# Three layers in one program block, idle TensorE time filled with transposes, and a mask moved ahead of a sigma

## The chip, the cores and the metric

The kernel runs on one core of one Trainium2 chip. The metric is the time of one execution on the device, in microseconds (us); less is better. A core has five engines that work side by side, each through its own list of instructions in order: TensorE (PE in the profile, its weight loads PEld), VectorE (DVE), ScalarE (ACT), GpSimd (POOL) and SyncE (SP), which here only issues transfers. An engine waits for another by a semaphore: the one counts it up at the end of an instruction, the other stands before an instruction until the count is reached. A float32 matmul here runs in passes over a 128 × 128 stationary operand. TensorE's clock has two levels, 1.2 and 2.4 GHz, and the profile shows the granted share of the full one: 0.5 is 1.2 GHz.

## What is computed

1024 tokens of 256 numbers pass through four layers, each taken of the normalised x and added to x. Cut to what matters:

```
x = x + delta_attention(layernorm(x))   # 16 heads of 128, segments of 64 tokens, a memory per head
x = x + mixture0(layernorm(x))          # "e0": 16 experts, 2 picked per token, and a shared expert
x = x + retention(layernorm(x))         # one head: Q, K turned by cos/sin tables, scores times a decay
x = x + mixture1(layernorm(x))          # "e1": 8 experts, the best one per token, weighted
```

In the first layer, per segment: `scores = q kT / sqrt(128)` masked causally, a softmax, `att_dot = softmax @ v`; `att_mem = sigma(q) @ mem / (sigma(q) @ z)` with `sigma(a) = elu(a) + 1`; then `mem += sigma(k)T @ (v - sigma(k) @ mem / (sigma(k) @ z))` and `z += sum of sigma(k)`. The output is a mix of the two by a sigmoid per head, times Wo. In the third layer, `Q = xpos(x W_Q)`, `K = xpos(x W_K)`, `att = (Q KT * D) V` with D a lower triangular decay.

## The kernel before

**The tiling.** Tokens lie in NT = 8 tiles of 128 partitions; a half is TPH = 4 tiles, 512 tokens. Float32 products that need precision are made of three matmuls, `split3` (L213 to L215), of a high and a low part of each operand. `Norm` serves the layernorm of every layer n (0 to 3) in halves: `statistics` and `normalise` (L132) on VectorE, `invert` (L112, the power −0.5) on GpSimd, `turn` (L140, eight transposes against the identity, two groups of four) on TensorE, `high` (L149, a copy) on ScalarE and `low` (L157, the difference) on VectorE. Each counts a semaphore, and the next waits for it.

**Attention** takes four heads at a time (`it`) and one half of the tokens (`half`): 8 stages, n = 0 to 7. A stage has 8 segments (STEPS) for two groups of two heads, so 16 recurrence steps, and behind each step `slot(it, half, m, ...)`, m = 0 to 15, issues other work on every engine: projections and sigma of the next stage ("ahead"), softmax and reading of this one. The order is written out by hand, in `AHEAD_AT` and in the slots' conditions. On VectorE `sigma(n + 1, ..., u)`, u = 0 to 7 (queries, then keys), is L869, L875 and, for keys, the copy L880; at m = 7 it is unit 5, the key of head 1. `mask_scores` (L907 and the row maximum L912) runs at m = 1 and m = 7, once for each pair of heads. TensorE's turn of the probabilities of the first pair into the bank `local` is L594, its turn of a key's sigma L554; ScalarE's L749 and L750 copy a projection (its exponent's input, and q or k) from a bank and L758 copies a turned sigma from one.

**The sparse layers** (`sparse_layer`, tag e0 or e1) turn the normalised rows, make router logits (`logits`, L1255 in e1), count the tokens of each expert (L1295 to L1302), number the slots (L1310), and then work through blocks of 128 gathered rows: a gather (L1195, GpSimd), a turn (L1331), gate and up (L1340, 128 × 352), the hidden's turn (L1350), down (L1358) and a scatter (L1206, GpSimd). `number_shares` (L1320) brings each row's weight into block order. In e0, SyncE reads the scattered results back and VectorE joins them to x (`join`, L1113): four calls, (half, k); (1, 1) is left to the retention (`join_last`).

**The retention** splits its three weights on GpSimd (`w_high` L1791, `w_low` L1795), projects Q and K in four units (`project`), multiplies each by cos and sin (`products`, L1921 and L1922 on VectorE), combines them on GpSimd (L1806), splits the outcome (L1885 on ScalarE, L1929 on VectorE), and makes scores and outputs tile by tile.

**What sets the order between layers.** Each of the four layers is an `nc.Block()`. At its end every engine drains (L1120) and all meet at a barrier; GpSimd's drain counts among them. Inside a block each engine works through what its function issues, in that order.

Of the kernel before, what the change touches and what calls it, by code (L numbers as in the profile page):

```python
# [165 lines left out]
class Carried:  # L166
# [3 lines left out]
    def __init__(self, nc, ctx):  # L170
# [9 lines left out]
        self.y_last = [flat[:, i * D:(i + 4) * D].rearrange("p (t d) -> p t d", d=D) for i in (12, 0)]  # L180
        self.tile_loaded = [sem(f"first_tile{i}_loaded") for i in range(2)]
# [3 lines left out]
class SharedTiles:  # L185
# [32 lines left out]
def delta_attention(nc, outer, norm, carried, x, ident, ident_ready, scratch, x_in, Wq, Wk, Wv, Wo, betas, mask_in,  # L218
# [12 lines left out]
    with ExitStack() as ctx:  # L231
# [114 lines left out]
        with nc.Block() as block:  # L346
# [497 lines left out]
            def _(dve):  # L844
# [58 lines left out]
                def mask_scores(n, before):  # L903
                    if before:
# [5 lines left out]
                       .then_inc(masked, 1)  # L910
                    dve.wait_ge(masked, n + 1)
# [77 lines left out]
def sparse_layer(nc, outer, norm, carried, x, ident, ident_ready, tag, experts, picks, w, tiles=None, next_w=None,  # L989
                 out=None, signals=()):  # L990
# [7 lines left out]
    with ExitStack() as ctx:  # L998
# [31 lines left out]
        consts = sb("consts", [P, table.shape[1]])  # L1030
# [7 lines left out]
        router = sb("router", [P, KD, E])  # L1038
# [45 lines left out]
        router_loaded, table_loaded, weights_loaded = sem("router_loaded"), sem("table_loaded"), sem("weights_loaded")  # L1084
# [23 lines left out]
        def join(engine, half, k):  # L1108
# [3 lines left out]
            for t in range(half * TPH, (half + 1) * TPH):  # L1112
                last = engine.scalar_tensor_tensor(  # L1113
# [6 lines left out]
        with nc.Block() as block:  # L1120
            @block.sync
            def _(sp):
# [3 lines left out]
                if out is not None:  # L1126
                    for half in range(2):
                        sp.dma_start(rows[half * HALF:(half + 1) * HALF, D:2 * D].rearrange("(t p) d -> p t d", p=P),
                                     x[:, half * TPH:(half + 1) * TPH, :]).then_inc(rows_stored, 16)
                if shared:  # L1130
                    tiles.load(sp, stage[2], 2, stage_loaded)
                for e in range(E):
                    sp.dma_start(weights[:, e, :], w["experts"][e, :, :]).then_inc(weights_loaded, 16)
                if shared:
                    for i in range(3):
                        sp.dma_start(carried.retention_w[i], next_w[i].rearrange("(k p) n -> p k n", p=P))\
                          .then_inc(carried.retention_w_loaded[i], 16)
                for ring in range(RING):
                    sp.wait_ge(scattered[ring], 16 * scatters(ring))
                if out is None:  # L1140
                    for half in range(2):
                        if half:
                            sp.wait_ge(y_loaded[0], 16 * K)
                        for k in range(K):
                            first = k * T + half * HALF
                            sp.dma_start(y[k][half], results[first:first + HALF, :].rearrange("(t p) d -> p t d", p=P))\
# [931 lines left out]
```

## Time and profile before

| | |
|---|---|
| time, median of 3 runs | 738.09 us (735.9 to 738.6) |
| the profiled execution | 737.92 us |
| its span, first to last instruction | 736.1 us |
| mean granted TensorE clock | 0.948 |
| busy TensorE, VectorE, ScalarE, GpSimd | 651.0, 401.8, 340.0, 317.1 us |
| attention | to 451.5 us |
| e0 | 451.5 to about 598 us |
| retention | 601.5 to about 656 us |
| e1 | 658.4 to 736 us |

The span is 1.8 us shorter than the execution, which has work around it. In the rows further down a line of a timeline is one instruction or a run of equal ones: its start, how long it was busy, engine, line, what it wrote and read; in square brackets how long the engine had idled before it, and what released it.

### The profile page before, as it was taken

The numbers are of one execution on the slowest core, as the hardware profiler recorded it, in microseconds if no ns is written. First come the engines' busy times: TensorE is split into PE (matmuls) and PEld (weight loads), VectorE is DVE, ScalarE is ACT, GpSimd is POOL, SyncE is SP. The second block draws the span as 40 slices with busy tenths as digits, with TensorE's granted clock in tenths as the row PEclk, the third lists the DMA queues.
The fourth block names the chain that finished last, engine by engine and source line by source line (L and its number), as shares of the span: only waits on it lengthen the run. The fifth ranks groups of instructions, "written<-read, shape, count | busy, mean of one in ns | idle before, by whom it ended". The sixth has DMA issues, their size and how long they took to land. (4 is left out here: it accounts for less than half of the span.)

```text
span 736.1 us, 12298 instructions
## 1 busy us (share of the span) xinstructions
PE 651.0 (88%) x4144; PEld 543.3 (74%) x4144; DVE 401.8 (55%) x1055; ACT 340.0 (46%) x834; POOL 317.1 (43%) x383
## 2 busy tenths in 40 slices
PE   4888999999999999999999987999999519984897
PEld 3777888989979979989889886875666317873564
DVE  6768396295394493691772737862222178354243
ACT  3565767467566565665765642233333203100210
POOL 4565562454353344436420204246665318111563
PEclk9999999999999999999999998999999859995799
DMA  8011010200200100100100414953232241019440
GB/s 265 23 54 34 29 55 5 63 31 2 65 29 22 44 28 28 36 28 29 37 1 1 115 53 137 415 189 93 93 91 76 100 148 53 1 56 341 134 124 15
DMA packets 31313, 57.89 MB, mean 79 GB/s; under 512 B 4670, under 2 KB 17952, under 8 KB 31264
## 3 DMA queue, kind: packets, MB, share of 16 engines
q1 hardware_dynamic: 24256, 42.03, 16.7%
q0 software_dynamic: 4896, 13.12, 6.1%
q10 hardware_dynamic: 2112, 2.10, 0.8%
q8 instruction: 29, 0.48, 0.3%
q14 instruction: 20, 0.16, 0.1%
HBM read 48.06 MB, written 10.09 MB: 79 GB/s over the span
## 5 line engine op out<-in xcount | busy, mean ns | idle before, releaser
L891 DVE RECIPROCAL denominators<-readings 128x2 f32<-128x2 f32 x128 | 21.1, 165 | 147.6 <-PE readings L567 146.6
L427 POOL TENSOR_TENSOR w_high<-xn,ones 128x256 fp32r<-128x256 f32 x84 | 53.9, 673 | 78.2 <-PE ahead L215 35.4
L567 PEld LDWEIGHTS readings<-memory_copy,sigma 128*128 128x128 f32 x512 | 75.2, 191 | 11.2 <-ACT memory_copy L764 2.1
L773 ACT ACTIVATE memory_reading<-readings,denominators 64x128 f32<-64x128 f32 x256 | 78.5, 356 | 6.0 <-DVE denominators L891 4.0
L567 PE MATMUL readings<-memory_copy,sigma 128*128 128x129 f32 x512 | 78.7, 275 | 2.2 <-ACT memory_copy L764 2.1
L764 ACT ACTIVATE memory_copy<-memory 128x258 f32<-128x258 f32 x128 | 50.2, 393 | 62.1 <-PE memory L577 48.1
L897 DVE SCALAR_TENSOR_TENSOR minus_delta<-readings,denominators,v 64x128 f32<-64x128 f32 x240 | 73.8, 347 | 4.5 <-DVE denominators L891 0.3
L577 PE MATMUL memory<-minus_delta,sigma_k_tokens 128*128 128x129 f32 x480 | 73.2, 275 | 0.0
L1195 POOL DMA_INDIRECT xs_e<-rows_e,gather_at_e x46 | 44.8, 974 | 58.4 <-DVE scatter_at_e L1596 36.1
L1340 PE MATMUL up_e<-weights_e,xT_e 128*128 x184 | 68.7, 497 | 0.8 <-ACT xT_e L1464 0.8
L431 POOL TENSOR_TENSOR w_low<-xn,w_high 128x256 fp32r<-128x256 f32 x84 | 65.7, 812 | 1.6
L616 PE MATMUL ahead<-wo,attT 128*128 128x256 f32 x256 | 64.5, 396 | 1.0 <-DVE attT L926 1.0
L749 ACT ACTIVATE x<-ahead 128x512 f32<-128x512 f32 x60 | 35.9, 598 | 61.5 <-PE ahead L215 28.3
L1681 DVE TENSOR_TENSOR h_e<-gated_e,up_e 128x176 f32<-128x176 f32 x46 | 15.5, 337 | 88.4 <-ACT gated_e L1471 88.4
L577 PEld LDWEIGHTS memory<-minus_delta,sigma_k_tokens 128*128 128x128 f32 x480 | 63.0, 191 | 0.0
L458 POOL TENSOR_TENSOR xn<-scores,exp_sum_inverse 64x512 f32<-64x512 f32 x32 | 34.1, 1065 | 60.8 <-DVE exp_sum_inverse L918 59.1
L616 PEld LDWEIGHTS ahead<-wo,attT 128*128 128x128 f32 x256 | 58.9, 306 | 1.3 <-DVE attT L926 1.2
L1358 PE MATMUL down_e<-weights_e,hT_e 128*128 (+1 forms) x184 | 56.3, 405 | 0.0
L213 PE MATMUL ahead<-xh,w_high 128*128 128x512 f32 x120 | 52.4, 437 | 1.9 <-POOL w_low L431 1.9
L449 POOL TENSOR_TENSOR scores<-scores,score_max 128x512 f32<-128x512 f32 x16 | 16.7, 1047 | 82.3 <-DVE score_max L912 76.6
L1340 PEld LDWEIGHTS up_e<-weights_e,xT_e 128*128 128x128 f32 x184 | 32.2, 195 | 24.9 <-issue 15.6
L215 PE MATMUL ahead<-xh,w_low 128*128 128x512 f32 x120 | 47.4, 395 | 0.0
(267 smaller groups left out, 1424.8 us busy)
## 6 DMA issues: line engine op xcount, KB each, us to landing
weights_e<-experts SPq DMA_DIRECT2D x24, 608.0 KB, 12.0
xn<-L_attn_Wq SPq DMA_DIRECT2D x8, 512.0 KB, 3.9
xn<-L_attn_Wk SPq DMA_DIRECT2D x7, 512.0 KB, 3.8
xn<-L_attn_Wv SPq DMA_DIRECT2D x7, 512.0 KB, 3.8
wo<-L_attn_Wo SPq DMA_DIRECT2D x1, 2048.0 KB, 13.1
rows_e<-xn ACTq DMA_DIRECT2D x4, 512.0 KB, 10.6
x<-L_attn_x SPq DMA_DIRECT2D x4, 256.0 KB, 3.5
x<-L_attn_x SPq DMA_DIRECT2D x2, 512.0 KB, 3.5
```

Of the source, the lines that this page charges most:

```text
L213: pe.matmul(out, sh, mh, start=first, stop=False, **kw)
L215: return pe.matmul(out, sl, mh, start=False, stop=last, **kw)
L427: last = pool.tensor_tensor(w_high[i][:, :, of], w_stage[:, :, of], one, ALU.mult)
L431: last = pool.tensor_tensor(w_low[i][:, :, of], w_stage[:, :, of], fr(w_high[i][:, :, of]), ALU.subtract)
L567: last = pe.matmul(KQ[g][:, hh * MC:(hh + 1) * MC], sqk[:, GROUP * g + hh, pair, 2 * par:2 * par + 2, :], mz[g][:, hh, :], start=True, sto ...
L577: last = pe.matmul(MM[g][:, hh * MC:(hh + 1) * MC], skt[:, GROUP * g + hh, pair, :], dl[g][par][:, hh, :], start=False, stop=True, skip_gr ...
L616: last = pe.matmul(A[1][:, 0:D], rows[:, i::H], wo[:, i, :], start=(i == 0), stop=(i == H - 1))
L764: act.activation(mz[g][:, :, :], MM[g][:, 0:GROUP * MC].rearrange("p (h c) -> p h c", h=GROUP), ACT.Copy).then_inc(mem_copied[g], 1)
L773: last = act.activation(read[rows, half, GROUP * g + hh, pair, :], KQ[g][rows, hh * MC:hh * MC + DK], ACT.Copy, scale=nr[g][rows, hh:hh + 1])
L897: last = dve.scalar_tensor_tensor(out=dl[g][par][rows, hh, 0:DK], in0=KQ[g][rows, hh * MC:hh * MC + DK], scalar=nr[g][rows, hh:hh + 1], in ...
L1340: last = pe.matmul(GU[b % 2][:, 0:2 * INTER], xT[b % 2][:, k, :], flat[:, bass.ds(first + k * 2 * INTER, 2 * INTER)], start=k == 0, stop=k ...
L1358: last = pe.matmul(Y[b % 2][:, 0:D], hT[b % 2][0:count, k, :], flat[0:count, bass.ds(first + 4 * INTER + k * D, D)], start=k == 0, stop=k ...
```

## The change

It has four parts.

1. **Attention.** `mask_scores` loses the row maximum, which becomes `row_maxima`. At m = 7 the mask is issued ahead of sigma unit 5, the row maximum stays behind it. At m = 1 nothing moves.
2. **Merged layers.** e0, the retention and e1 are bodies of one block, made with `no_gpsimd_drain=True`: no drain and no barrier stands between them, and none of GpSimd behind them. Three waits order what the barriers did: SyncE's loads of the retention's tables wait for the read-back of e0 (`read_back`), e1's row stores wait for the retention's last addition (`earlier_done`), and e1's router and table are loaded inside the retention, into `carried`, once its second normalise is done.
3. **Filled time.** `busy` issues transposes of the identity into a bank that nobody reads: 16 before and 14 after the retention's first turn, 16 after e1's first logits, 8 after its second turn, 34 after its slot numbers.
4. **Order.** Both inversions of the retention's layernorm stand on GpSimd behind its weight splits (the first one was in e0). VectorE's last two joins are cut in halves, around a normalise and around a `low`. TensorE projects the second unit before the second turn, not behind it; `number_shares` comes behind the first block's gate and up matmuls.

The diff, with changed indentation left out:

```diff
+def busy(pe, bank, ident, count):
+    for _ in range(count):
+        pe.transpose(bank[:, 0:P], ident[:, :], ident[:, :])
...
+                def row_maxima(n):
                     dve.wait_ge(masked, n + 1)
                     dve.tensor_reduce(mx[:, :], sm[:, :, :], AX.X, ALU.max).then_inc(max_ready, 1)
...
                     ahead, behind = not (last and half), not (first and not half)
+                    if m == 7:
+                        mask_scores(2 * n + 1, True)
                     if ahead:
...
+                    if m == 1:
+                        mask_scores(2 * n, behind)
                     if m in (1, 7):
-                        mask_scores(2 * n + m // 7, behind or m == 7)
+                        row_maxima(2 * n + m // 7)
...
-        with nc.Block() as block:
             @block.sync
             def _(sp):
+            if out is None:
                 sp.dma_start(router[:, :, :], w["router"].rearrange("(k p) e -> p k e", p=P))\
                   .then_inc(router_loaded, 16)
                 sp.dma_start(consts[:, :], table).then_inc(table_loaded, 16)
-                if out is not None:
+            else:
+                sp.wait_ge(earlier_done, 4)
...
-                if out is None:
-                    norm.invert(pool, N + 1, 0)
...
                     logits(0)
+                busy(pe, acc[0], ident, 16)
                     norm.turn(pe, N, 1, acc)
+                busy(pe, acc[0], ident, 8)
                     logits(1)
                     count_tokens()
                     number_slots()
+                busy(pe, acc[0], ident, 34)
...
-                if out is not None:
-                    number_shares()
                 turn_rows(0)
                 turn_rows(1)
...
                         block_gate_up(b, firsts[b])
+                if out is not None and b == 0:
+                    number_shares()
...
-                    join(dve, 1, 0)
+                join(dve, 1, 0, (0, 1))
                     norm.normalise(dve, N + 1, 0)
+                join(dve, 1, 0, (2, 3))
...
+            sp.wait_ge(read_back, 16 * K0)
                 for i, t in enumerate(tables):
                     sp.dma_start(cos_sin[:, i, :], t).then_inc(tables_loaded, 16)
                 sp.dma_start(decay[:, :], decay_in).then_inc(decay_loaded, 16)
+            sp.wait_ge(norm.xn_done, NT * 2 + TPH)
...
-                    if i == 0:
-                        pool.wait_ge(w_split, 1)
-                        norm.invert(pool, 2, 1)
-                        pool.wait_ge(norm.xn_done, NT * 2 + NT)
+            for half in range(2):
+                norm.invert(pool, 2, half)
...
-                pe.wait_ge(ident_ready, 2)
+            pe.wait_ge(norm.stats_done, NT * 2 + 1)
+            busy(pe, B[7], ident, 16)
                 norm.turn(pe, 2, 0, B[0:4])
+            busy(pe, B[7], ident, 14)
...
                 project(0)
-                norm.turn(pe, 2, 1, B[0:4])
                 project(1)
+            norm.turn(pe, 2, 1, B[0:4])
...
-                join_last(dve)
+            join_last(dve, (0, 1))
                 norm.low(dve, 2, 0, B[0:4])
+            join_last(dve, (2, 3))
...
+        with nc.Block(no_gpsimd_drain=True) as block:
```

**Where the instructions stand.** VectorE in an attention stage's slot 7, before. `x` is the exponent that sigma caps, `scores` the masked scores, `score_max` the row maxima, `local0` the bank of the raw scores:

```order
L897 SCALAR_TENSOR_TENSOR minus_delta11<-readings1,denominators1,v 64x128 x2
L869 TENSOR_SCALAR x<-x 128x512
L875 SCALAR_TENSOR_TENSOR sigma_k1<-kT,x 128x512
L880 COPY sigma<-sigma_k1 128x4x2x64
L907 SCALAR_TENSOR_TENSOR scores<-local0,mask 128x512
L912 TENSOR_REDUCE score_max<-scores 128x8
```

The same place after:

```order
L908 SCALAR_TENSOR_TENSOR minus_delta11<-readings1,denominators1,v 64x128 x2
L918 SCALAR_TENSOR_TENSOR scores<-local0,mask 128x512
L880 TENSOR_SCALAR x<-x 128x512
L886 SCALAR_TENSOR_TENSOR sigma_k1<-kT,x 128x512
L891 COPY sigma<-sigma_k1 128x4x2x64
L925 TENSOR_REDUCE score_max<-scores 128x8
```

The mask has moved up over the three instructions of one sigma, and the row maximum has not.

GpSimd from e0's last scatters to the retention's rotations, before (`rstd` is an inversion; `w_low_r` and `w_high_r` are the weight splits):

```order
L1206 DMA results_e0<-ys2_e0,scatter_at_e0 6016x256
L112 TENSOR_TENSOR rstd<-var_eps,power 128x4
L1120 UNCONDITIONAL_BRANCH
L1784 UNCONDITIONAL_BRANCH
L1786 MEMSET ones_r 128x1
L1795 TENSOR_TENSOR w_low0_r<-carried,w_high0_r 128x512
L112 TENSOR_TENSOR rstd<-var_eps,power 128x4
L1791 TENSOR_TENSOR w_high1_r<-carried,ones_r 128x512
L1795 TENSOR_TENSOR w_low1_r<-carried,w_high1_r 128x512
L1791 TENSOR_TENSOR w_high2_r<-carried,ones_r 128x512
L1795 TENSOR_TENSOR w_low2_r<-carried,w_high2_r 128x512
L1806 TENSOR_TENSOR turned0_r<-product0_r 128x512 x2
```

The same place after:

```order
L1228 DMA results_e0<-ys2_e0,scatter_at_e0 6016x256
L1813 UNCONDITIONAL_BRANCH
L1815 MEMSET ones_r 128x1
L1824 TENSOR_TENSOR w_low0_r<-carried,w_high0_r 128x512
L1820 TENSOR_TENSOR w_high1_r<-carried,ones_r 128x512
L1824 TENSOR_TENSOR w_low1_r<-carried,w_high1_r 128x512
L1820 TENSOR_TENSOR w_high2_r<-carried,ones_r 128x512
L1824 TENSOR_TENSOR w_low2_r<-carried,w_high2_r 128x512
L112 TENSOR_TENSOR rstd<-var_eps,power 128x4 x2
L1833 TENSOR_TENSOR turned0_r<-product0_r 128x512 x2
```

The block's end (L1120) is gone from between them, and both inversions stand behind all five splits.

TensorE at the front of e1, before:

```order
L1777 UNCONDITIONAL_BRANCH
L1229 UNCONDITIONAL_BRANCH
L140 MATMUL down_e<-ident,xn 128x128 x8
L1255 MATMUL routing_e<-router_e,turned_e 128x8 x8
L140 MATMUL down_e<-ident,xn 128x128 x8
L1255 MATMUL routing_e<-router_e,turned_e 128x8 x8
```

The same place after:

```order
L1249 UNCONDITIONAL_BRANCH
L140 MATMUL down_e<-ident,xn 128x128 x8
L1275 MATMUL routing_e<-carried,turned_e 128x8 x8
L218 MATMUL down_e<-ident 128x128 x16
L140 MATMUL down_e<-ident,xn 128x128 x8
L218 MATMUL down_e<-ident 128x128 x8
L1275 MATMUL routing_e<-carried,turned_e 128x8 x8
```

L218 are the transposes of the identity: they stand between the first logits and the second turn, and between that turn and the second logits.

## Rows read from the trace of the kernel before

**Rows 1.** The page's line of the granted TensorE clock, in 40 slices, in tenths.

```profile
PEclk9999999999999999999999998999999859995799
```

**Rows 2.** Waits, 60 to 540 us: who waited for whom, us, times, longest.

```profile
PE local L594 <- DVE scores L907: 6.2, 7, 2.7
```

**Rows 3.** Timeline of an ordinary attention stage: start, duration, engine, line, [idle <-releaser].

```profile
270.06 0.69 DVE L907 SCALAR_TENSOR_TENSOR scores<-local,mask 128x512 f32<-128x512 f32 x1
270.06 0.60 ACT L749 ACTIVATE x<-ahead 128x512 f32<-128x512 f32 x1 [0.67 <-DVE sigma L880]
270.55 0.59 ACT L750 ACTIVATE kT<-ahead 128x512 f32<-128x512 f32 x1
...
270.81 1.09 PE L594 MATMUL local<-ident,xn 128*128 128x128 f32 x8 [0.57 <-DVE scores L907]
271.03 0.60 ACT L758 ACTIVATE sigma_k_tokens<-ahead 128x512 f32<-128x512 f32 x1
...
271.74 0.60 PE L554 MATMUL ahead<-ident,sigma_k 128*128 128x128 f32 x4
...
272.09 0.48 PE L213 MATMUL ahead<-w_high,xh 128*128 128x512 f32 x1
```

**Rows 4.** Timeline of the first attention stage.

```profile
64.47 0.60 ACT L749 ACTIVATE x<-ahead 128x512 f32<-128x512 f32 x1 [2.06 <-DVE sigma L880]
...
65.30 0.69 DVE L907 SCALAR_TENSOR_TENSOR scores<-local,mask 128x512 f32<-128x512 f32 x1 [0.93 <-POOL xn L458]
...
66.14 1.86 PE L594 MATMUL local<-ident,xn 128*128 128x128 f32 x8 [2.72 <-DVE scores L907]
...
67.80 1.06 PE L554 MATMUL ahead<-ident,sigma_k 128*128 128x128 f32 x4
```

**Rows 5.** The drains that end a block: durations min/median/max in ns.

```profile
L1120 SPq DRAIN  x2: 7/64/122, 590.4 to 734.8; - x2
L1120 POOLq DRAIN  x2: 3757/5000/6242, 595.0 to 732.2; - x2
```

**Rows 6.** Timeline from the first sparse layer to the retention.

```profile
595.16 1.67 DVE L1113 SCALAR_TENSOR_TENSOR x<-y_e,carried,x 128x256 f32<-128x256 f32 x4 [0.24 <-DMA carried<-results_e]
...
601.57 2.68 DVE L1113 SCALAR_TENSOR_TENSOR x<-carried,x 128x256 f32<-128x256 f32 x4 [3.43 <-PEq L1120]
...
605.62 0.79 PE L213 MATMUL bank_r<-xh,w_high_r 128*128 128x512 f32 x1 [2.05 <-DVE xl L157]
```

**Rows 7.** Timeline of the retention: rotary products, rotations, first score matmul.

```profile
612.53 0.68 DVE L1921 TENSOR_TENSOR product_r<-bank_r,cos_sin_r 128x512 f32<-128x512 f32 x1
...
614.74 6.06 POOL L1806 TENSOR_TENSOR turned_r<-product_r 128x512 f32<-128x512 f32 x4
...
627.15 0.50 PE L213 MATMUL bank_r<-q_high_r,k_high_r 128*128 128x512 f32 x1 [0.43 <-DVE q_low_r L1929]
```

**Rows 8.** Timeline from the retention to the second sparse layer.

```profile
655.28 1.38 DVE L132 TENSOR_SCALAR xn<-x,mean_var,rstd 128x256 f32<-128x256 f32 x4 [0.16 <-POOL rstd L112]
...
658.55 1.06 PE L140 MATMUL down_e<-ident,xn 128*128 128x128 f32 x8 [2.40 <-PEq L1777]
...
660.45 3.55 PE L1255 MATMUL routing_e<-router_e,turned_e 128*128 128x8 f32 x16 [0.83 <-ACT turned_e L1437]
```

**Rows 9.** Windows: us, busy PE PEld DVE ACT POOL, PEclk, DMA share, GB/s.

```profile
70.00:72.00 2.00, 2.00 (x16) 1.86 (x16) 0.80 (x4) 0.98 (x2) 0.00 (x0) 1.00 0.00 0
...
660.00:661.00 1.00, 0.56 (x3) 0.58 (x3) 0.26 (x3) 0.30 (x1) 0.63 (x1) 0.58 1.02 302
```

**Rows 10.** Timeline of the second sparse layer, up to its third block.

```profile
677.11 0.39 PE L1310 MATMUL routing_e<-token_e,in_slot_e 128*128 128x30 bf16 x8 [4.43 <-DVE token_e L1581]
...
684.32 0.69 PE L1331 MATMUL routing_e<-ident,xs_e 128*128 128x128 f32 x2 [0.79 <-DMA xs_e<-rows_e,gather_at_e]
...
685.82 2.71 PE L1340 MATMUL up_e<-weights_e,xT_e 128*128 x4 [0.81 <-ACT xT_e L1464]
...
691.43 1.35 PE L1340 MATMUL up_e<-weights_e,xT_e 128*128 x4
```

More of the change, by code:

```diff
@@ L1029, in sparse_layer @@
         table = w["table"]
-        consts = sb("consts", [P, table.shape[1]])
+        consts = carried.next_table if out is not None else sb("consts", [P, table.shape[1]])
         at = table_columns(E, K)
@@ L1106, in sparse_layer, with join @@
         turned_done = sem("turned_done")
-        def join(engine, half, k):
+        def join(engine, half, k, part=range(TPH)):
             engine.wait_ge(y_loaded[half], 16 * K)
@@ L1111, in join @@
                 engine.wait_ge(joined, (half * K + k) * TPH)
-            for t in range(half * TPH, (half + 1) * TPH):
-                last = engine.scalar_tensor_tensor(
+            for t in (half * TPH + i for i in part):
+                engine.scalar_tensor_tensor(
                     out=x[:, t, :], in0=y[k][half][:, t - half * TPH, :], scalar=share[:, k, t:t + 1],
@@ L1134, in _ @@
-                if shared:
[L1135 to L1139, printed above, removed]
-                if out is None:
[L1141 to L1146, printed above, removed]
-                              .then_inc(y_loaded[half], 16)
@@ L1727, in join_last @@
-    def join_last(engine):
-        join(engine, 1, 1)
-        engine.wait_ge(joined, 2 * K * TPH)
-    return join_last
-def retention(nc, outer, norm, carried, x, ident, ident_ready, tables, decay_in, join_last):
+            else:
+                sp.wait_ge(earlier_done, 4)
+                for half in range(2):
+                    sp.dma_start(rows[half * HALF:(half + 1) * HALF, D:2 * D].rearrange("(t p) d -> p t d", p=P),
+                                 x[:, half * TPH:(half + 1) * TPH, :]).then_inc(rows_stored, 16)
@@ L1740, in retention, with join_last @@
+    def join_last(engine, part):
+        join(engine, 1, 1, part)
+        if TPH - 1 in part:
+            engine.wait_ge(joined, 2 * K * TPH)
+    return join_last, y_loaded[1]
+def retention(block, nc, outer, norm, carried, x, ident, ident_ready, tables, decay_in, join_last, read_back, next_w):
     with ExitStack() as ctx:
@@ new lines, in _, with high, copy_v @@
+        @block.scalar
+        def _(act):
+            act.wait_ge(w_loaded[0], 16)
+            act.activation(w_high[0][:, :, :], w_stage[0][:, :, :], ACT.Copy).then_inc(high_done, 1)
+            for half in range(2):
+                norm.high(act, 2, half, B[0:4])
+            def high(u):
+                qk, half = units[u]
+                act.wait_ge(turn_done, 2 * u + 2)
+                act.activation(qk_high[qk][:, :, half * HALF:(half + 1) * HALF], turned[u % 2][:, :, :], ACT.Copy)\
+                   .then_inc(qk_high_done, 1)
+            def copy_v(b):
+                act.wait_ge(v_ready, 2 * b + 2)
+                act.activation(v[:, 2 * b:2 * b + 2, :], B[4 + b][:, :].rearrange("p (t d) -> p t d", t=2), ACT.Copy)\
+                   .then_inc(v_copied, 1)
+            high(0)
+            high(1)
+            copy_v(0)
+            copy_v(1)
+            high(2)
+            copy_v(2)
+            copy_v(3)
+            high(3)
@@ L1965, in build @@
+        return added
 def build(nc, ins, out):
```

1340 lines of the change are left out of this document (669 added, 671 removed).

## Prediction

> **What bounds the kernel now.** Three views are read, in this order. The page's line of the granted TensorE clock comes first: nearly full in the attention stages (the first 451 us, 24 slices), at half in slice 33 (589 to 607 us: the end of the first sparse layer and the front of the retention), and at 5 and 7 tenths in slices 37 and 38 (662 to 699: the front of the second sparse layer) [rows 1]. Those dips are the places that the merge and the fillers touch. The waits of the attention stages come next: the matmul that turns the second pair's probabilities (L594) waits for the mask (L907) on VectorE seven times, 6.2 us in total, 2.7 of it once [rows 2]. The timelines around each changed place are last. In attention TensorE is busy nearly all the time, so an instruction that reaches it late is paid; behind attention the path runs from engine to engine, and each edit is read from the wait that ends last there. All is worked against the profiled execution, 737.92 us, of which the span is 736.1 and 1.8 lie around it. It is 0.2 below the median of the runs shown (738.09), so a change of the one is a change of the other.
>
> **Attention, +3.1 us.** In an ordinary stage the mask ends at 270.75, the turn L594 starts at 270.81 having idled 0.57, takes 1.09, and the key's turn L554 follows at 271.74, the projection of the next stage at 272.09 [rows 3]. With the mask first, L594 no longer idles, but the key's sigma ends 0.72 later (0.69 and a gap). Three things hang on that sigma. ScalarE's copy L749 is released by it: 270.06 becomes 270.78. The copy L750 behind it reads the bank that L554 writes, and ends at 271.86 instead of 271.14; L554 then starts at about 271.90, not 271.74, though TensorE is free 0.57 sooner. The copy L758 ends at 272.35 instead of 271.63, and the projection's bank waits for it: 272.40 instead of 272.09, +0.31. So the removed wait comes back on the next two instructions, with 0.31 on top. Six such stages are +1.9. In the first one the mask had to wait 0.93 for GpSimd's L458, until 65.30, while the sigma before it had let L749 go at 64.47 [rows 4]. The sigma now queues behind that wait: it starts when the mask ends, at 65.99, and L749 behind it moves by some 2 us. TensorE idled there anyway until 66.14 [rows 4], so the end that all of it hides is +0.4 and the end that all is paid is +2.1; +1.2 is taken, the middle, for nothing decides. The last stage has no sigma. The sum is 1.9 + 1.2 = +3.1. Were the waits simply to go and nothing to take their place, it would be at best 6 × 0.57 = −3.4, say −3.5; the upper bound, with the first stage at its upper end and 0.4 per stage, is +4.5.
>
> **First sparse layer to retention, −4.2 us.** GpSimd's drain starts at 595.0 and takes 6.2 [rows 5]; the other engines stand at the barrier until 601.4, VectorE for 3.43 [rows 6]. Without it the order is: the last inversion, then the first two joins (0.42 each, 1.67 for four [rows 6]), normalise at 596.1 for 1.38 (as long as in [rows 8]), the turn on TensorE at 597.5. The 16 transposes ahead of it fill idle time, and the 14 behind it lie beside ScalarE's two copies and VectorE's differences; the other joins cost 0.42, not 0.67 (2.68 for four [rows 6]), because no split runs beside them. The first projection starts at 600.5 instead of 605.62 [rows 6]. Two units of projection run before the second turn (24 matmuls, to 606.0), and VectorE is free for the rotary products at 608.5 instead of 612.53 [rows 7]. GpSimd takes them up at 609.8 instead of 614.74: it was behind the weight splits, which now lie in its idle time before 595. From there eight rotations set the pace; a little slower beside products, they deliver the last at about 622.7 where the first score matmul stood at 627.15 [rows 7], −4.4. TensorE, done earlier, now idles some 2.8 us before the scores where it idled 0.43, and may lose its clock: 0.2 is set aside, and the bounds are −4.6 and −2.9 (1.7 for a stretch at 1.2 GHz). The new wait of SyncE, for the read-back, is over when the joins start at 595.16, and the tables then have 12 us to land. That the second turn now stands behind the second projection is in the 608.5.
>
> **Front of the second sparse layer, −2.1 us.** The normalise ends at 656.66, and the turn came at 658.55, released by the barrier [rows 8]; it now comes at 656.7, and the first logits at 658.5 instead of 660.45, −1.95. The clock was at 1.2 GHz in 660 to 661, after this idling [rows 9], and the 16 logits matmuls took 3.55 [rows 8] without raising it. The 16 transposes cost 16 × 0.135 = 2.2 at the upper level (1.06 for eight [rows 8]) and 16 × 0.23 = 3.7 at the lower (1.86 for eight [rows 4]); the next 8 lie beside ScalarE's copies (0.83 of idle ahead of the first logits [rows 8]) and cost 0.3 net. At the upper level the second turn takes 0.9 less and the second logits about 1.7 less, half of 3.55, an estimate. If the clock falls in the first logits and is up again by the end of the 16: −1.95 + 3.7 + 0.3 − 0.9 − 1.7 = −0.6. If it never falls, the first logits save 1.7 too: −1.95 + 2.2 + 0.3 − 0.9 − 3.4 = −3.8. About the middle is taken. Router and table are now loaded in the retention; no row here waits for them, so that is nothing. Upper bound 0.
>
> **First expert blocks, −1.8 us.** The slot numbers are done at 677.5, and until the first rows land TensorE has the 24 share matmuls and nothing else; the second set is turned at 684.32, the first gate and up matmuls start at 685.82 and take 2.71, where the same takes 1.35 at 691.43 [rows 10]. The 34 transposes start at 677.5; with the clock low for the first 3.5 (in attention it was low from 66.14 and full from 70 on [rows 4, 9]) they are done at 683.6 (15 × 0.23, 19 × 0.135), before the second set's rows at 684.32. Then the first two blocks run at the upper level: 2 × 1.35 saved, less 0.5 for the 24 share matmuls, now between them, and less what the blocks wait for ScalarE's table load; the third block starts at 689.7 instead of 691.43. Bounds: −2.2, and +1.4, when the clock rises late.
>
> **The end, −1.1 us.** GpSimd's drain from 732.2 takes 3.8, to 736.0; SyncE, which waits for the stores of the result, is done at 734.8 [rows 5]. Bounds 0 and −1.1.
>
> **Sum.** 3.1 − 4.2 − 2.1 − 1.8 − 1.1 = −6.1, so 731.8 for the profiled execution and 732.0 beside the median.
>
> **A rule against it.** From 66.14 on TensorE had turns alone, eight in 1.86 at the lower level and four more to 68.9 [rows 4], and from 70 to 72 the clock was full [rows 9], so turns may help to raise it. The Trainium skill, "TensorE: Matmul & The Clock Gate", Part 4 (PE-mode transpose), says that such a transpose "doesn't count as PE-busy the same way". By it the fillers would be pure cost, as in rival 2.
>
> **Rivals.** 1: *the attention's wait goes and nothing takes its place* (the copies turn out not to hold the banks that I think). Attention −3.5 in place of +3.1: 731.8 − 6.6 = 725.2, so 725.4 beside the median. For it: L594's wait is real. Against it: L749 is released by the sigma in both stages shown [rows 3, 4]. Chance 0.07. 2: *the fillers do not raise the clock* and end above the kernel before. The retention's front keeps −1.2, since 14 transposes at 0.23 hold its first projection back by 3.2 and only the rotations' earlier start is left; the second layer's front is −1.95 + 24 × 0.23 − 0.7 = +2.9; 34 × 0.23 = 7.9 puts the first turned rows to 685.4, and with the shares behind them that is +2.1; attention +3.1, end −1.1. The sum is +5.8, 744. It decides from the point at which the 34 end later than the rows land, 684.3, which is 0.20 per transpose. For it: the first logits kept the clock low for all their length [rows 8]. Against it: the turns of [rows 4]. Chance 0.09. 3: *the clock falls in the longer idle of the retention, or rises late in the second layer*: retention −2.9, front 0, blocks −0.3 or worse: 735 to 737. For it: idling of 2.4 was enough before 660 [rows 8, 9], and 2.8 are expected here. Chance 0.19. 4: *a data wait takes the barrier's place* (the read-back, the splits or the stores end as late as the drain did), and with attention's loss nothing is left: 738. Against it: the joins' data had landed at 595.16 [rows 6]. Chance 0.05. The forecast keeps 0.60.
>
> **How the numbers follow.** The likeliest is 732.0. Its own range, from the bounds of the terms that can fall apart without a rival, is 728.5 to 734.4. The range to hold 8 in 10 takes in most of rival 3 and rival 4: 727.5 to 738.5; outside lie rival 1, rival 2 and little else. About 0.5% is what a measurement of this kernel can tell from no change: faster ends at 734.4, slower begins at 741.8. Forecast and rival 1 are faster, 0.67; rivals 3 and 4 are within, 0.24; rival 2 is slower, 0.09.
>
> **What would show it.** In attention, the wait of L594 for the mask gone and waits of the key's turn and of the projection for ScalarE's copies in its place, and a stage 0.3 longer; if it is shorter, that step is wrong. The first projection of the retention at 600.5 and GpSimd's first rotation at 609.8. A clock at 2.4 GHz from the 16 transposes to the scores. In the second layer, the 34 transposes finished within 6.1 us, and the first gate and up matmuls at 1.35, not 2.71. The last store, not a drain, as the end. What would make the prediction wrong: turns that do not raise the clock, a stage's end set by another chain than ScalarE's copies, or a GpSimd that reaches the last inversion late.

## The result, and the profile after

The changed kernel takes 733.9 us (median of 9 runs, 732.1 to 735.7), the kernel before 738.05 beside it (9 runs). The ratio is 0.9948, 95% interval 0.9932 to 0.9964: 0.5% faster, 4.15 us. The profiled execution has a span of 732.1, 4.0 less than before. The forecast was 732.0, so the direction and the range held, and a third of the gain was missing. Stages of the same code differ in length from one profiled execution to the next, so where one execution misleads, several are compared below.

The page of the changed kernel gives this granted clock. Against [rows 1], slice 33 (586 to 604 us here) stands at 6 instead of 5, and slices 37 and 38 at 6 and 9 instead of 5 and 7; slice 4, in the first attention stage, stands at 8 instead of 9:

```profile
PEclk9998999999999999999999999899999969996999
```

The same places in the two profiled executions, read from the timelines; a place is the start of the instruction named:

| place | before | after | change | change since the place above |
|---|---|---|---|---|
| GpSimd's first softmax difference, stage 0 | 52.28 | 50.83 | −1.45 | −1.45 |
| first transfer of the first sparse layer | 451.57 | 453.64 | +2.07 | +3.52 |
| last variance of that layer (L126) | 594.75 | 597.22 | +2.47 | +0.40 |
| retention's first projection | 605.62 | 603.12 | −2.50 | −4.97 |
| its rotary products | 612.53 | 611.17 | −1.36 | +1.14 |
| GpSimd's first rotation | 614.74 | 612.53 | −2.21 | −0.85 |
| first score matmul | 627.15 | 624.92 | −2.23 | −0.02 |
| normalise at its end | 655.28 | 654.60 | −0.68 | +1.55 |
| second layer's turn | 658.55 | 656.12 | −2.43 | −1.75 |
| first gate and up matmuls | 685.82 | 684.34 | −1.48 | +0.95 |
| those of the third block | 691.43 | 688.42 | −3.01 | −1.53 |
| end of the span | 736.1 | 732.1 | −4.0 | −1.0 |

The first line is not the change's: over the fourteen profiled executions of this study that place lies anywhere between 50.8 and 53.6.

**Attention.** The waits of TensorE for the mask, and for ScalarE's copy of a projection, from 90 to 450 us, first of the kernel before:

```profile
PE local L594 <- DVE scores L907: 3.5, 6, 0.6
PE ahead L554 <- ACT kT L750: 2.1, 6, 0.4
```

and of the changed kernel, where the only one of the kind is:

```profile
PE ahead L565 <- ACT kT L761: 6.2, 12, 0.7
```

The mask's wait is gone, and the key's turn waits twice as often, 6.2 us instead of 2.1. The ordinary stage of [rows 3], in the changed kernel:

```profile
269.66 0.69 DVE L918 SCALAR_TENSOR_TENSOR scores<-local,mask 128x512 f32<-128x512 f32 x1
...
271.32 1.04 PE L605 MATMUL local<-ident,xn 128*128 128x128 f32 x8
...
271.90 0.60 ACT L760 ACTIVATE x<-ahead 128x512 f32<-128x512 f32 x1 [1.26 <-DVE sigma L891]
...
272.40 0.59 ACT L761 ACTIVATE kT<-ahead 128x512 f32<-128x512 f32 x1
...
273.04 0.66 PE L565 MATMUL ahead<-ident,sigma_k 128*128 128x128 f32 x4 [0.69 <-ACT kT L761]
...
273.53 0.49 PE L224 MATMUL ahead<-w_high,xh 128*128 128x512 f32 x1
```

L605 (L594 before) ends at 272.36 and TensorE then stands 0.69 until L761 has read the bank at 272.99. One stage, from one difference of GpSimd to the one two further, is 271.55 − 219.50 = 52.05 before and 272.54 − 220.24 = 52.30 after. First the two lines of the kernel before, then those of the changed one:

```profile
219.50 1.04 POOL L449 TENSOR_TENSOR scores<-scores,score_max 128x512 f32<-128x512 f32 x1 [5.05 <-DVE score_max L912]
...
271.55 1.04 POOL L449 TENSOR_TENSOR scores<-scores,score_max 128x512 f32<-128x512 f32 x1 [5.05 <-DVE score_max L912]
```

```profile
220.24 1.04 POOL L460 TENSOR_TENSOR scores<-scores,score_max 128x512 f32<-128x512 f32 x1 [4.80 <-DVE score_max L925]
...
272.54 1.04 POOL L460 TENSOR_TENSOR scores<-scores,score_max 128x512 f32<-128x512 f32 x1 [4.79 <-DVE score_max L925]
```

**Retention.** The rows that answer to [rows 6, 7]:

```profile
595.99 3.67 PE L218 MATMUL bank_r<-ident 128*128 128x128 f32 x16 [12.59 <-DVE stats L120]
...
601.51 1.69 PE L218 MATMUL bank_r<-ident 128*128 128x128 f32 x14
...
603.12 0.51 PE L224 MATMUL bank_r<-xh,w_high_r 128*128 128x512 f32 x1
...
611.17 0.68 DVE L1951 TENSOR_TENSOR product_r<-bank_r,cos_sin_r 128x512 f32<-128x512 f32 x1
...
612.53 6.06 POOL L1833 TENSOR_TENSOR turned_r<-product_r 128x512 f32<-128x512 f32 x4 [5.66 <-DVE product_r L1952]
...
624.92 0.63 PE L224 MATMUL bank_r<-q_high_r,k_high_r 128*128 128x512 f32 x1 [2.10 <-DVE q_low_r L1959]
```

The sixteen transposes run at 0.23 each, the fourteen behind the turn at 0.12, and the first projection starts at the full clock, 0.51 instead of 0.79. But the first score matmul has 2.10 of idle time before it (0.43 in [rows 7]) and takes 0.63 instead of 0.50. The windows around it (us, busy time of the five engines, PEclk, DMA share, GB/s):

```profile
623.00:625.00 2.00, 0.08 (x1) 0.08 (x1) 1.87 (x2) 1.38 (x3) 2.00 (x2) 1.00 0.00 0
625.00:627.00 2.00, 2.00 (x5) 1.57 (x6) 0.00 (x0) 0.97 (x1) 1.00 (x1) 0.53 0.00 0
627.00:629.00 2.00, 2.00 (x7) 1.57 (x6) 1.83 (x2) 0.09 (x1) 0.00 (x0) 0.61 0.00 0
629.00:631.00 2.00, 2.00 (x11) 1.68 (x10) 0.77 (x2) 0.00 (x0) 0.00 (x0) 1.00 0.00 0
```

The clock fell at 625.1, behind the idling, and was back at 628.6: that is the +1.55 of the table.

**The second sparse layer**, against [rows 8, 10]:

```profile
656.12 1.06 PE L140 MATMUL down_e<-ident,xn 128*128 128x128 f32 x8 [0.66 <-DVE xn L132]
...
658.02 2.42 PE L1275 MATMUL routing_e<-carried,turned_e 128*128 128x8 f32 x16 [0.83 <-ACT turned_e L1460]
...
660.29 3.65 PE L218 MATMUL down_e<-ident 128*128 128x128 f32 x16
...
663.73 1.92 PE L140 MATMUL down_e<-ident,xn 128*128 128x128 f32 x8
...
666.64 1.85 PE L1275 MATMUL routing_e<-carried,turned_e 128*128 128x8 f32 x16
...
675.79 5.83 PE L218 MATMUL down_e<-ident 128*128 128x128 f32 x34
...
684.34 1.45 PE L1360 MATMUL up_e<-weights_e,xT_e 128*128 x4 [1.09 <-ACT xT_e L1487]
```

The first logits took 2.42: the clock fell to the lower level at 659.3, inside them. The sixteen ran at 0.23 each, the second turn at the lower level too (1.92), and the clock was back only at 666.1, so just the second logits were short again. The first gate and up matmuls take 1.45, not 2.71.

### The profile page after: what moved, and what is told of

It is laid out like the page before. It is cut to its first block and busy times, and to the rows that moved or that the text cites. A ratio compares the mean times of both kernels' runs of the same rounds, so it can differ in the third digit from the quotient of the medians.

```text
span 732.1 us, 12452 instructions
## 1 busy us (share of the span) xinstructions
PE 659.9 (90%) x4232; PEld 552.9 (76%) x4232; DVE 399.3 (55%) x1055; ACT 339.8 (46%) x834; POOL 316.1 (43%) x383
## 5 line engine op out<-in xcount | busy, mean ns | idle before, releaser
L1360 PE MATMUL up_e<-weights_e,xT_e 128*128 x184 | 66.9, 487 | 1.1 <-ACT xT_e L1487 1.1
L760 ACT ACTIVATE x<-ahead 128x512 f32<-128x512 f32 x60 | 35.9, 598 | 67.8 <-DVE sigma L891 30.7
```

The lines of the kernel that those rows point to most:

```text
L1360: last = pe.matmul(GU[b % 2][:, 0:2 * INTER], xT[b % 2][:, k, :], flat[:, bass.ds(first + k * 2 * INTER, 2 * INTER)], start=k == 0, stop=k ...
```

## Experiments

All ratios are to the kernel before, run beside each experiment, with a 95% interval; the changed kernel's is 0.9948 (0.9932 to 0.9964). It was not run again beside them, so a distance from the changed kernel is a difference of two ratios, and known to some 2 us at best.

**Attention alone.** The kernel before with the edits of slot 7.

```diff
+                    if m == 7:
+                        mask_scores(2 * n + 1, True)
...
-                        mask_scores(2 * n + m // 7, behind or m == 7)
+                        if m == 1:
+                            mask_scores(2 * n, behind)
+                        row_maxima(2 * n + m // 7)
```

> The kernel before with the attention's reordering alone. The prediction's step: +3.1 us (six ordinary stages at +0.31, the first stage at +1.2), so a ratio of 1.0042. By the trace of the changed kernel an ordinary stage is 0.25 longer and attention as a whole 2.1: +2.1, ratio 1.0028, if that execution's shorter start is the kernel's own; +3.4, 1.0046, if its first 52 us were shorter by chance. Rival (the removed wait simply goes): -3.5, 0.995. In its trace the mask's wait of L594 is gone and the key's turn waits for ScalarE's copy instead.

Measured: 1.0034 (1.0015 to 1.0052), +2.5 us. The stages are as long as in the changed kernel (five of 52.36 on average against 52.12 before, the last 0.52 longer). The reordering is a loss, of about the size expected.

**All but attention.** The changed kernel with slot 7 as before.

```diff
-                    if m == 7:
-                        mask_scores(2 * n + 1, True)
...
+                        mask_scores(2 * n + m // 7, behind or m == 7)
```

> The changed kernel with slot 7 as before. If the attention's reordering costs what the step says, this is 2.1 to 3.4 us below the changed kernel: 730.5 to 731.8, ratio to the kernel before 0.990 to 0.992. Rival (the reordering is neutral, the missing gain is elsewhere): 733.9, ratio 0.995.

Measured: 0.9903 (0.9875 to 0.9930), 0.45% or 3.3 us below the changed kernel. The reordering costs what was expected of it, and the neutral rival is out.

**An earlier release of ScalarE's copy**, to tell why. ScalarE writes the exponent of unit u into the buffer that unit u − 2 used. VectorE's last read of it is the sum L886; the copy L891 behind it touches it no more, but ScalarE waited for that.

```diff
-                        if u >= 2:
+                        if u >= 6:
+                            act.wait_ge(sk_ready, 4 * n + u - 5)
+                        elif u >= 2:
                             act.wait_ge(sigma_ready, 8 * n + u - 1)
```

> The changed kernel in which ScalarE's copy of the last two key projections (units 6 and 7) waits for VectorE's last read of the exponent two units before, instead of for the copy of sigma behind that read: 0.46 earlier each. Theory (the mask-first order makes that copy, and the bank it holds, the thing that the key's turn waits for): 0.46 less on the second turn of each stage and 0.34 on the first, some 0.6 to 0.8 times 7: 4.2 to 5.6 below the changed kernel, ratio 0.987 to 0.989, the mask-first order now costing nothing against the other. Rival (something else in the stage is what the reordering delays, VectorE's own queue or the row maximum): at most 1 below the changed kernel, ratio 0.994.

> The same earlier release with slot 7 in the old order (sigma ahead of the mask). Theory: only the first turn of each stage gains (0.34), since the second stands behind the wait for the mask anyway: 2.4 below the changed kernel in the old order (ratio 0.990), so 0.987. The distance between the two orders, 0.45% without the earlier release, shrinks to nothing or turns round. Rival: the distance stays at 0.45%.

Measured: mask first 0.9923 (0.9899 to 0.9948), sigma first 0.9900 (0.9872 to 0.9928). The first is 1.8 us below the changed kernel, where 4.2 to 5.6 were expected; the second is where the old order stood without the release (0.9903). The totals can't decide between the orders, since the first sparse layer alone, up to its last variance, took 146.8 in the profiled execution of the one and 142.2 in that of the other, with the same code. The ordinary stages can. Mask first, 271.58 − 219.78 = 51.80:

```profile
219.78 1.04 POOL L460 TENSOR_TENSOR scores<-scores,score_max 128x512 f32<-128x512 f32 x1 [4.79 <-DVE score_max L927]
...
271.58 1.05 POOL L460 TENSOR_TENSOR scores<-scores,score_max 128x512 f32<-128x512 f32 x1 [4.79 <-DVE score_max L927]
```

Sigma first, 271.34 − 219.25 = 52.09, no shorter than the 52.05 without the release:

```profile
219.25 1.05 POOL L460 TENSOR_TENSOR scores<-scores,score_max 128x512 f32<-128x512 f32 x1 [5.04 <-DVE score_max L927]
...
271.34 1.05 POOL L460 TENSOR_TENSOR scores<-scores,score_max 128x512 f32<-128x512 f32 x1 [5.04 <-DVE score_max L927]
```

Their waits from 90 to 450 us, first mask first, then sigma first:

```profile
PE ahead L565 <- ACT kT L763: 4.1, 6, 0.7
```

```profile
PE local L605 <- DVE scores L920: 6.2, 6, 1.1
```

With the release, the ordinary mask-first stage loses 0.50 and the two orders change places: it is now 0.29 shorter than the other. In the old order whatever the earlier copy gives is handed over to the wait for the mask, which grows from 3.5 (the wait shown above of the kernel before) to 6.2. So in an ordinary stage the delay of ScalarE's copy is what the reordering cost. The expectation of a gain on the first turn in the old order (0.34 per stage) was wrong for that reason.

The layer as a whole is another matter. From GpSimd's first softmax difference to its last, which leaves the chance of the start out, it is:

| order, release | executions | us |
|---|---|---|
| sigma first, as before | 2 | 364.7 and 364.8 |
| sigma first, earlier release | 1 | 364.8 |
| mask first, as in the changed kernel | 8 | 367.5 to 368.3 |
| mask first, earlier release | 3 | 364.9 to 365.1 |

The release gives back about 3, all of the reordering's cost and no more. The first stage stays 1.6 to 1.8 longer than in the old order (44.24 to 44.39 against 42.54 to 42.64), and that eats what the ordinary stages gain. What makes the first stage longer with the release in place, no run shows.

**No transposes at all.**

```diff
-            busy(pe, B[7], ident, 16)
...
-            busy(pe, B[7], ident, 14)
...
-                busy(pe, acc[0], ident, 16)
...
-                busy(pe, acc[0], ident, 8)
...
-                busy(pe, acc[0], ident, 34)
```

> The changed kernel without any of the 88 transposes of the identity. Theory (they raise the clock and sit in idle time, but the 24 in the second layer's front pay for themselves only): the retention's first projections run at 1.2 GHz, +1.6, the front 0, the first gate and up matmuls at 1.2 GHz, +1.4: 736.9, ratio 0.998. Rival 2 of the prediction (transposes of the identity do not raise the clock, they only cost): faster than the changed kernel by 2 to 3, 731.

Measured: 1.0000 (0.9983 to 1.0016), 3.8 us above the changed kernel, where 3.0 were expected. Rival 2 is out: without the transposes the merge only pays for the attention's loss. The kernel's first projection starts 6.5 behind the last variance, and the products 16.3 (5.9 and 13.95 in the changed kernel):

```profile
606.85 0.80 PE L224 MATMUL bank_r<-xh,w_high_r 128*128 128x512 f32 x1 [1.41 <-DVE xl L157]
...
616.67 0.68 DVE L1946 TENSOR_TENSOR product_r<-bank_r,cos_sin_r 128x512 f32<-128x512 f32 x1
```

**One batch at a time.** Each of the three takes out the named lines of the diff above: the retention's 16 + 14, the second layer's 16 + 8, and its 34.

> The changed kernel without the 16 + 14 transposes at the retention's first turn. From the trace of the kernel without any of the 88: the rotary products start 2.4 later behind the last statistics of the first sparse layer (16.3 instead of 13.9), and nothing behind it catches up: 2.4 above the changed kernel, ratio 0.998. Rival 2 of the prediction (transposes of the identity bring no clock) expects it to be no slower than the changed kernel: 0.995.

> The changed kernel without the 16 + 8 transposes at the front of the second sparse layer. From the traces: without the 16 the second turn starts 1.6 earlier (its normalise ends at 662.1), at 1.2 GHz, and the second logits take 3.58 instead of 1.85, so the logits end within 0.3 of the changed kernel's; the 34 transposes then start at the lower level as they did there. Expected: no difference from the changed kernel, ratio 0.995 plus or minus 0.001. The prediction's step (the 24 bring 2.1 less 1.95 of the barrier's) says the same. Rival (the clock is what they save): 2 above.

> The changed kernel without the 34 transposes behind the slot numbers. The step of the prediction: the first two blocks' gate and up matmuls run at 1.2 GHz, 2.71 and 2.42 instead of 1.45 and 1.35; the third block comes 1.4 to 1.8 later: ratio 0.997. Rival (what the blocks wait for is ScalarE and the gathers, not the clock): 0 to 0.5, ratio 0.995.

Measured: 0.9986 (0.9963 to 1.0008), 0.9960 (0.9941 to 0.9980), 0.9984 (0.9964 to 1.0005), so 2.8, 0.9 and 2.7 us above the changed kernel, each known to some 2. They add up to 6.4, where all three batches together gave 3.8; with such errors that is no contradiction, but the three values can't be added. Without the retention's 30 the products start 16.2 behind the last variance, as without any (16.3). Of the 34 the trace says why: without them the first two blocks ran at the lower level.

```profile
687.11 2.71 PE L1360 MATMUL up_e<-weights_e,xT_e 128*128 x4 [0.84 <-ACT xT_e L1486]
...
691.05 2.20 PE L1360 MATMUL up_e<-weights_e,xT_e 128*128 x4
...
693.52 1.35 PE L1360 MATMUL up_e<-weights_e,xT_e 128*128 x4
```

For the 24 the totals allow anything from nothing to 3 us, and one execution misleads. In that of the changed kernel the logits end 13.9 behind the layer's normalise, and without the 24 they end at 13.8: worth nothing, it seems. But of the nine profiled executions with all 24 only two (the changed kernel, and the one without the 34) are like that. In the other seven the logits end at 12.3. Here one of them, the kernel with the earlier release:

```profile
658.91 3.14 PE L218 MATMUL down_e<-ident 128*128 128x128 f32 x16
...
661.85 1.55 PE L140 MATMUL down_e<-ident,xn 128*128 128x128 f32 x8
...
664.10 1.93 PE L1277 MATMUL routing_e<-carried,turned_e 128*128 128x8 f32 x16
```

Its clock was low from 659.5 to 662.9, for 3.4 us; in the changed kernel's execution it was low for 6.8, from 659.3 to 666.1, under the same work. So the 24 bring 1.5 there in seven cases of nine, and the third block comes at 33.9 to 34.1 behind the normalise in these, against 35.4 in the one execution without the 24.

**Transposes ahead of the scores.**

```diff
+            pe.wait_ge(prod_done, 6)
+            busy(pe, B[0], ident, 14)
             scores(0)
```

> The changed kernel with 14 more transposes of the identity between the retention's last v matmul and its first score matmul, where TensorE idled 2.1 us and its clock fell to 1.2 GHz until 628.6. Theory (the fall there is what took 1.5 of the retention's gain): the score matmuls start at 2.4 GHz and the time is 1.5 less, 732.4, ratio 0.9925. Rival (the scores' front is set by VectorE and GpSimd, which the clock does not touch): 733.9, unchanged, ratio 0.995.

Measured: 0.9920 (0.9898 to 0.9943), 2.0 us below the changed kernel where 1.5 were expected, though the two intervals overlap. The first score matmul takes 0.50 again, and the retention from there to its last normalise 28.1, not 29.7:

```profile
623.37 1.69 PE L218 MATMUL bank_r<-ident 128*128 128x128 f32 x14
...
625.65 0.50 PE L224 MATMUL bank_r<-q_high_r,k_high_r 128*128 128x512 f32 x1 [0.59 <-DVE q_low_r L1961]
```

Whether the clock falls there without them is not fixed: of the nine profiled executions of merged kernels without these fourteen it fell in seven (29.7) and held in two (28.1); with them it held in three of three.

**GpSimd's drain put back.**

```diff
-        with nc.Block(no_gpsimd_drain=True) as block:
+        with nc.Block() as block:
```

> The changed kernel with GpSimd's drain back at the end of its one block. The prediction's last step (the end, -1.1): 1.0 above the changed kernel, ratio 0.996, and the last instruction of the trace is the drain, 3.7 long. Rival (the drain waits for what the last stores wait for anyway): no difference, 0.995.

Measured: 1.0040 (1.0014 to 1.0065), 0.92% or 6.8 us above the changed kernel, over six times what was expected. GpSimd's drain at the end of this kernel; the columns are those of [rows 5]:

```profile
L2023 POOLq DRAIN  x1: 8824/8824/8824, 730.3 to 730.3; - x1
```

It takes 8.8 us. Before, there were two, of 6.2 behind 31 gathers and 31 scatters, and of 3.8 behind 15 and 15 [rows 5]; the merged block has all 92. The three durations rise by 0.08 us for each indirect transfer since the last drain (6.24 − 3.76 over 32, 8.82 − 3.76 over 62). Two blocks without any, attention and the retention of the kernel before, have drains of 2.0 and 1.1. No run changed the number of transfers alone: that their number is the cause is read off these durations and not shown.

**Both findings together.** The changed kernel with the earlier release and the transposes ahead of the scores; then the same with 10 in place of 16 between the second layer's first logits and second turn.

> The changed kernel with both findings: ScalarE's earlier release in attention (stages of 51.94 us, not 52.40: 7 times 0.46, 3.2 less) and the 14 transposes ahead of the retention's first score matmul (1.5 to 2 less). If they add up, ratio to the kernel before 0.9948 less 0.0043 less 0.0025, 0.988. Rival: either gain is absorbed behind attention by ScalarE's late copy at the second sparse layer's first blocks, and the ratio is 0.991 or more.

> As the kernel with both findings, but 10 transposes, not 16, between the second layer's first logits and second turn: in the traces the second turn's input is ready 1.0 before the 16 end. Expected 0.6 to 0.9 less than with 16, ratio 0.987; rival: with fewer the clock is still at 1.2 GHz in the second turn and logits, and it is 0 to 1 more.

Measured: 0.9879 (0.9835 to 0.9923) and 0.9880 (0.9839 to 0.9921). The first is 731.0 us beside 739.8 for the kernel before, as expected, and faster than both kernels. Against the changed kernel with the old order of slot 7 (0.9903) it is not: the intervals overlap, and the attention of the two is equally long by the table above. The old order with the 14 transposes ahead of the scores was not run. As for the second kernel, expected 0.6 to 0.9 below the first, the six fewer transposes make no difference that this can tell. In the traces they do let the logits end 0.4 earlier behind the normalise (11.9, not 12.3).

## Why the prediction was right, and where it was too high

**Attention: right, by its own steps.** +3.1 was the sum; the two traces show +3.5 (with the chance of the start left out), the two comparisons +2.5 and +3.3. ScalarE's chain was at the named places: its two copies of the key's projection late (L760, L761), the key's turn behind them, the next projection behind that. Five of the six ordinary stages lost 0.25 and the last 0.52, together 1.8 where 1.9 was reckoned; the first lost 1.7, not 1.2: near the upper bound, TensorE's idling there hid little. In the profiled execution the shorter start hides 1.45 of the +3.5.

**First layer to retention: right up to the scores.** Counted from the last variance (+2.47): the first projection −4.97 for −5.1, the products −3.83 for −4.0, GpSimd's first rotation −4.68 for −4.9, the first score matmul −4.70 for −4.4. Behind it, a term that was too small: 0.2 was set aside for the clock in the longer idling (2.10 and not the 2.8 reckoned), and it cost 1.55. The fall is a case that comes or does not, and it came in seven executions of nine; the prediction had it within rival 3, at 0.19. The term's own bound, −2.9, held the −3.15 that was measured.

**Front of the second layer and first blocks: −2.3 for −3.9.** From the normalise to the third block it was 36.15 and is 33.82. That is the largest miss. The barrier's part was right (−1.75 for −1.95 on the turn). The first logits kept a good part of the clock, but in the changed kernel's execution the sixteen transposes ran wholly at the lower level (3.65), and the second turn too, where 2.2 to 3.7 and a turn at the upper level were reckoned. The logits' end moved by −0.9 there, near −0.6, the case in which the clock falls and comes back. In the seven other executions named above it moved by −2.5 (12.3 against 14.8 before), more than the −2.1 of "about the middle". One reading of this term was off: in the kernel before the clock did not fall in the idling of 2.4. The turn behind it still took 1.06 for eight, and the 0.58 of [rows 9] holds the fall, at 660.2. The 34 were right: 5.83 for the 6.1 given, the blocks at 1.45 and 1.35. Yet in those seven executions the third block comes no earlier (33.9 to 34.1), so there it is the first blocks' −1.8 that failed: the front gained 2.5 and the blocks behind it gained nothing.

There is a limit behind this that the prediction did not see. In the nine other kernels with the 34, the first gate and up matmuls come at 27.7 to 29.6 behind the normalise (29.7 in the changed kernel), and yet the third block at 33.6 to 35.4 (33.8). The rows of the kernel with transposes ahead of the scores (its third block's gate and up matmuls start at 687.84):

```profile
683.25 0.32 ACT L1494 ACTIVATE gated_e<-up_e 128x176 f32<-128x176 f32 x1 [0.83 <-PE up_e L1360]
...
683.99 0.41 PE L1351 MATMUL gate_e<-ident,xs_e 128*128 128x128 f32 x2 [0.18 <-issue]
...
686.97 0.17 DVE L1579 COPY slot_share_e<-down_e 128x15 f32<-128x15 f32 x1 [9.37 <-remote]
687.01 0.38 ACT L1487 ACTIVATE xT_e<-gate_e 128x256 f32<-128x256 f32 x1 [3.44 <-PE routing_e L1351]
```

ScalarE's copy of the third block's rows starts at 687.01, 2.6 after TensorE had turned them, though ScalarE had nothing before it since 683.57. It is not ScalarE alone: VectorE's copy of the shares (L1579), whose matmuls end at 683.81, is held for 3.16, and in all nine executions it is held for 2.8 to 3.2 and starts 0.04 ahead of ScalarE's. In the program both wait for counts of TensorE only. What holds them, the profile doesn't say, and no run was spent on it; the profiled execution of the changed kernel is the only one of the ten in which the copy followed the turn at once. This stays open, and it is where up to 2 us of what an earlier front brings go.

**The end: right.** −1.0 for −1.1. But the step named the smaller part of what the flag does: it was priced against the drain of 3.8 that the old block had, and the merged block would have had one of 8.8. Without the flag the change would have been slower than the kernel before (1.0040).

**The rivals.** That transposes do not raise the clock is refuted. From 596 to 603 TensorE ran only the 16, the eight of the turn and the 14, with 0.33 of idling between, and the windows show its clock:

```profile
596.00:598.00 2.00, 2.00 (x10) 2.00 (x11) 1.80 (x10) 0.00 (x0) 0.53 (x1) 0.50 0.29 100
...
601.00:603.00 2.00, 2.00 (x19) 1.96 (x17) 1.94 (x5) 1.16 (x2) 0.00 (x0) 0.94 0.97 381
```

The level rises from 0.50 to 0.94 on float32 transposes of 128 × 128 alone. For these the sentence of the Trainium skill, "TensorE: Matmul & The Clock Gate", Part 4, that a PE-mode transpose "doesn't count as PE-busy the same way", does not hold; the measurement decides. That attention's wait would simply go (rival 1) is refuted by both attention runs, and no data wait took the barrier's place (rival 4): the joins started 0.16 after the variance.

**The sum.** −4.0 in the spans is −1.45 of chance at the start, +3.5 for attention, +0.4 in the first sparse layer, −3.15, −2.3 and −1.0. Against the forecast's −6.1, 1.6 are lost in the front and the first blocks of the second layer, 1.05 in the retention (1.35 of clock, less 0.3 won ahead of it), 0.9 in attention, the first sparse layer and the end; the short start gives 1.45 back.

## What to carry to other kernels

When an instruction is moved ahead of another on an in-order engine, price the one that now waits by following who it releases: here 0.57 of TensorE's waiting went, and 0.72 on VectorE came back through ScalarE's hold on a bank as 0.25 more per stage. Shortening the next link too (a wait on the last read of a buffer, not on the instruction behind it) turned it into a gain in the ordinary stages, but over the whole layer it only paid the loss back, and that link alone brought nothing. The old order did as well without either. Idle time that arises on TensorE in front of a wait should be filled, or priced with what a fall of the clock costs in full (1.55 here, in seven executions of nine), not with a small allowance (0.2). Where a term has two cases, as the clock's fall has, read several executions: the changed kernel's own showed the rarer case at the second layer's front. And where blocks are merged, look at what each block's end pays for: GpSimd's drain was the longer the more had been gathered and scattered before it.

## What was not expected of the hardware

- GpSimd's drain was longer with more indirect transfers since the one before: 3.8 us behind 30, 6.2 behind 62, 8.8 behind 92, and 1.1 and 2.0 behind none.
- Transposes of the identity (float32, 128 × 128) bring TensorE's clock up by themselves, and 14 of them, 1.7 us, in a gap of 2.1 kept it up in three executions of three, where it fell in seven of nine without.
- Under the same transposes at the second layer's front the clock stayed low for 3.4 us in one execution and for 6.8 in another.
- VectorE and ScalarE were held for about 3 us together, and released within 0.04 us of each other, in nine executions of ten at the same place.
- The same code of the first sparse layer, up to its last variance, took from 142.2 to 146.8 us in the profiled executions, which is more than most effects here; stages had to be read one by one.
